# Joining two programs of a Trainium2 kernel into one, with a LayerNorm run by pairs of tiles behind the last residual sums

## The chip, the cores and the metric

The kernel runs on one core of one Trainium2 chip. The metric is the device time of one execution in microseconds; the kernel before takes 2159.62 us (median of 3 runs, 2158.93 to 2162.39). Inside the core TensorE (PE), VectorE (DVE), ScalarE (ACT), GpSimd (POOL) and SyncE (SP, which here issues every DMA) run in parallel and meet at semaphores.

## The reference, cut to what matters

`x` is 1024 tokens (2 batches of 512) by 512. Four residual layers follow each other, each fed by a LayerNorm without weights:

```
x = x + (block-masked linear)(layernorm(x))     # 512 -> 512, with bias
x = x + ffn(layernorm(x))                       # int4-like weights, dequantized by groups of 128
x = x + mixer(layernorm(x))                     # Mamba-2 style, 128 heads of 64
x = x + ffn(layernorm(x))                       # the same weights again

layernorm(x) = (x - mean(x)) / sqrt(var(x) + 1e-5)
ffn(x)   = (silu(x @ Wg) * (x @ Wu)) @ Wd       # W = (q - z) * s, inner width 1792
mixer(x): proj = x @ in_proj.T                  # gate, x, B, C, dt
          dt = softplus(dt + dt_bias); conv of 4 taps and silu on x, B, C
          chunked scan over 4 chunks of 128 tokens; RMS norm, gate, out_proj
```

Inputs of floating type and the output are fp32.

## The kernel before, in words

Tokens are 8 tiles of 128 (`T = 8`), held in SBUF as `xr`. Every product of fp32 accuracy is three fp32r matmuls (`PASSES`: high by high, high by low, low by high), so each operand has a "high" copy, rounded by ACT, and a "low" copy, the remainder, made by DVE or POOL.

There are two programs (`nc.Block`), both written by the function `ffn(name, tiles, dst, lead, ...)`, with a barrier of all engines between them. The first ("f1") leads with the masked linear layer (class `Mixing`) and then runs the FFN; the second ("f2") leads with the mixer (class `Mixer`, 64 steps of the loop over `k`, one pair of heads and one batch each) and then runs the FFN again. In each program every engine has its own list of instructions, in an order written by hand.

The FFN works on 14 tiles of the inner width, two at a time: `PAIRS = 7` bodies. A body has, on PE, gate and up projections of two inner tiles over two halves of the tokens (96 matmuls, L406), then for each token tile t a down projection of 6 matmuls (L417) into one of four banks `dn_bank[t % 4]`. On DVE it has `deq_dn` and `deq_gu` (dequantize the next weights, two passes each, L264, L269, L248, L255), `hidden` (L276, L279) and the eight residual sums `xr += dn_bank` (L303). The down projection of tile t waits until the sum of tile t - 4 has read the bank; in the first body (`first`) only tiles 4 to 7 wait. The first body starts after the norm in front of it, so its DVE list is shifted against the PE's: both `deq_gu(p + 1, ...)` stand before the sums there.

In the last body of f1 each sum is followed by `mixer_stats(t)` (BN_STATS of the tile, L460). SP stores each finished tile to `x_mid` in DRAM (L241) and waits for all eight stores; then the program ends.

The mixer then starts with its own norm: on DVE eight BN_AGGR, the variance, a reciprocal after ACT's square root (L1268, with a table load), and for each tile `m_xn = (x - mean) * rstd` (L1490); PE turns each tile with 4 transposes (`turn_norm`, L1080), ACT makes the high copy (L1262), DVE the low copy (L1475). On PE follow `project_dt(0)` and `project_dt(1)` (L1088, 12 matmuls each) and the projections of the units b, c, x, z (12 matmuls each, `project`, L958). ACT's `tap` (L1214) and three DVE passes (`conv`, L1379) make the convolution of a unit. The chain of `dt` is: DVE adds the bias (L1498), takes -|dt| (L1501), ACT takes exp (L1279) and ln(1 + .) (L1282, another table), DVE forms `dt_h` (L1505), and PE turns it (`turn_dt`, L1097), after which `cumulate` (L1104), the cumulative sums and their stores and loads through DRAM lead to step 0 of the mixer.

The norm inside f1 and f2 already goes by pairs, with helpers of which these are the ones that the change reuses: `norm_var(i)` (two BN_AGGR and the addition of eps, L94 to L98), `norm_root` (ACT square root, L103), `norm_inverse` and `norm_shift` (DVE, L108 and L113), `norm_center_act` (ACT, `x * rstd + shift`, L121), `norm_turn` (PE, L129), `norm_high` (ACT, L135) and `norm_low` (DVE, L141).

Of the kernel before, what the change touches and what calls it, by code (L numbers as in the profile page):

```python
# [5 lines left out]
P = 128  # L6
F32 = mybir.dt.float32
# [40 lines left out]
def build(nc, x_in, mask_t, wa_t, bias_a, w_in, conv_w, conv_b, dt_bias, a_log, d_res, norm_w, w_out,  # L48
          gu_w, gu_z, gu_s, dn_w, dn_z, dn_s, x_mid, e_t, a_parts, out):
    with ExitStack() as ctx:  # L50
# [23 lines left out]
        class Norm:  # L74
            def __init__(self, name, sb, x, banks):
                self.x, self.lnt, self.xn, self.banks = x, None, None, banks
# [40 lines left out]
        def norm_center_act(act, n, t):  # L117
            act.wait_ge(n.stats_done, 7 * (t // 2) + 7)
            if t >= 2:
                act.wait_ge(n.turned, t - 1)  # L120
            nc.scalar.activation(n.xn[:, t % 2], n.x[:, t], ACT.Identity, bias=n.shift[:, t:t + 1],  # L121
                                 scale=n.rstd[:, t:t + 1]).then_inc(n.xn_done, 1)

        def norm_turn(pe, n, t):
            pe.wait_ge(n.xn_done, t + 1)
            if t >= 4:
                pe.wait_ge(n.lo_done, t - 3)
            for k in range(KT):
                last = nc.tensor.transpose(n.banks[t % 4][:, k * P:(k + 1) * P],  # L129
                                           n.xn[:, t % 2, k * P:(k + 1) * P], ident[:])  # L130
            last.then_inc(n.turned, 1)

        def norm_high(act, n, t):
            act.wait_ge(n.turned, t + 1)
            nc.scalar.activation(n.lnt[:, 0, :, t * P:(t + 1) * P],  # L135
                                 n.banks[t % 4][:].rearrange("p (k c) -> p k c", k=KT),
                                 ACT.Copy).then_inc(n.hi_done, 1)

        def norm_low(dve, n, t):
            dve.wait_ge(n.hi_done, t + 1)  # L140
            nc.vector.tensor_tensor(n.lnt[:, 1, :, t * P:(t + 1) * P],  # L141
                                    n.banks[t % 4][:].rearrange("p (k c) -> p k c", k=KT),
# [61 lines left out]
        def ffn(name, tiles, dst, lead, also_load=None, also_after=None):  # L204
# [11 lines left out]
            dn_mm, res_done, stored = sem(name + "_dn_mm"), sem(name + "_res_done"), sem(name + "_stored")  # L216
            g_bank, u_bank, dn_bank = tiles.banks[0:2], tiles.banks[2:4], tiles.banks[4:8]
# [8 lines left out]
            with nc.Block() as block:  # L226
                @block.sync
                def _(sp):
                    lead.sync(sp, tiles)
                    with sp.Fori(1, PAIRS) as p:  # L230
                        for j in range(2):
                            sp.wait_ge(gu_deq, 2 * p + (j - 1))
                            tiles.load_gu(sp, p, j)
                        for j in range(2):
                            sp.wait_ge(dn_deq, 2 * p + (j - 1))
                            tiles.load_dn(sp, p, j)
                    if also_load:
                        also_load(sp)
                    for t in range(T):
                        sp.wait_ge(res_done, (PAIRS - 1) * T + t + 1)  # L240
                        sp.dma_start(dst[t * P:(t + 1) * P, :], xr[:, t]).then_inc(stored, 16)  # L241
                    sp.wait_ge(stored, 16 * T)

                @block.vector
                def _(dve):
                    def sub_gu(p, j):
                        dve.wait_ge(gu_loaded[j], 48 * p + 48)
                        nc.vector.tensor_tensor(gu_q[j][:].bitcast(F32), gu_q[j][:], gu_zr[j][:], ALU.subtract)\  # L248
                            .then_inc(gu_sub, 1)

                    def scale_gu(p, j):
                        dve.wait_ge(gu_sub, 2 * p + (j + 1))
                        if not (isinstance(p, int) and p == 0 and j == 0):
                            dve.wait_ge(gu_lo, 2 * p + j)
                        nc.vector.tensor_tensor(gu_f[:], gu_q[j][:].bitcast(F32), gu_sr[j][:], ALU.mult)\  # L255
                            .then_inc(gu_deq, 1)

                    def deq_gu(p, j):
                        sub_gu(p, j)
                        scale_gu(p, j)  # L260

                    def deq_dn(p, j, first):
                        dve.wait_ge(dn_loaded[j], 48 * p + 48)
                        nc.vector.tensor_tensor(dn_q[:, j].bitcast(F32), dn_q[:, j], dn_zr[:, j], ALU.subtract)\  # L264
                            .then_inc(dn_sub, 1)
                        dve.wait_ge(dn_sub, 2 * p + (j + 1))
                        if not first:
                            dve.wait_ge(dn_lo, 2 * p + j)
                        nc.vector.tensor_tensor(dn_f[:], dn_q[:, j].bitcast(F32), dn_sr[:, j], ALU.mult)\  # L269
                            .then_inc(dn_deq, 1)  # L270

                    def hidden(p, j, half):
                        u = 2 * j + half
                        dve.wait_ge(u_mm, 4 * p + (u + 1))
                        dve.wait_ge(silu_done, 4 * p + (u + 1))
                        nc.vector.tensor_tensor(hf[:, half], silu[:, half], u_bank[half][:], ALU.mult)\  # L276
                            .then_inc(hf_done, 1)
                        dve.wait_ge(h_hi, 4 * p + (u + 1))
# [1477 lines left out]
```

## Time and profile before

| what | value |
|---|---|
| median of 3 runs | 2159.62 us (2158.93 to 2162.39) |
| time of the profiled execution | 2159.47 us |
| its span on the core | 2157.7 us |
| mean granted TensorE clock | 0.993 of full |
| PE busy | 2110.9 us, 98% |
| DVE, ACT, POOL busy | 1693.8, 1393.3, 881.9 us |
| DMA moved | 241.89 MB |

The profile describes one execution. Busy time of PE is not PE at its peak: matmuls at a lower granted clock count as busy too. The masked linear layer and the first FFN take the span up to about 286 us, the mixer up to about 1916 us, the second FFN the rest.

### The profile page before, as it was taken

The numbers are of one execution on the slowest core, as the hardware profiler recorded it, in microseconds if no ns is written. First come the engines' busy times: TensorE is split into PE (matmuls) and PEld (weight loads), VectorE is DVE, ScalarE is ACT, GpSimd is POOL, SyncE is SP. The second block draws the span as 40 slices with busy tenths as digits, with TensorE's granted clock in tenths as the row PEclk, the third lists the DMA queues.
The fourth block names the chain that finished last, engine by engine and source line by source line (L and its number), as shares of the span: only waits on it lengthen the run. The fifth ranks groups of instructions, "written<-read, shape, count | busy, mean of one in ns | idle before, by whom it ended". The sixth has DMA issues, their size and how long they took to land.

```text
span 2157.7 us, 37467 instructions
## 1 busy us (share of the span) xinstructions
PE 2110.9 (98%) x13386; PEld 1736.3 (80%) x13386; DVE 1693.8 (78%) x2682; ACT 1393.3 (65%) x1901; POOL 881.9 (41%) x622
## 2 busy tenths in 40 slices
PE   7999988999999999999999999999999999999999
PEld 6788867788888888888888888888888888877887
DVE  7555467989898888888898889898887988875554
ACT  5322247878787778777787877787777778742221
POOL 1222124445454544454454544544544545422221
PEclk9999989999999999999999999999999999999999
DMA  5544214333333333233323333333333233354441
GB/s 200 164 144 141 68 65 129 113 99 97 109 99 98 109 99 117 95 104 108 99 99 108 103 95 116 104 121 95 99 105 107 92 111 98 112 184 155 138 146 39
DMA packets 128644, 241.89 MB, mean 112 GB/s; under 512 B 14048, under 2 KB 48608, under 8 KB 128224
## 3 DMA queue, kind: packets, MB, share of 16 engines
q1 hardware_dynamic: 128480, 239.73, 35.1%
q8 instruction: 100, 1.64, 0.3%
q14 instruction: 64, 0.52, 0.1%
HBM read 234.17 MB, written 5.51 MB: 111 GB/s over the span
## 4 chain that ended last, share of the span: by engine, by line
PE 80%; DVE 2%; issue 2%; ACT 1%; DMA 1%; POOL 0%; SPq 0%; DVEq 0%; ACTq 0%; POOLq 0%
PE ring L958 35%; PE ring L1058 15%; PE bank_e L406 6%; PE yt L1039 6%; PE st L1023 4%; PE yt L1045 4%; PE bank_e L417 3%; PE xt L1010 3%; PE arg L996 2%; PE xt L971 1%; DMA w_raw<-w_in 0%; PE arg L1088 0%; DVE xc L1379 0%; PE st L983 0%; DVE m_xn L1490 0%
## 5 line engine op out<-in xcount | busy, mean ns | idle before, releaser
L958 PE MATMUL ring<-m_lnt,w_sb 128*128 128x512 f32 x3456 | 860.6, 399 | 1.9 <-DVE xc L1379 1.9
L958 PEld LDWEIGHTS ring<-m_lnt,w_sb 128*128 128x128 f32 x3456 | 632.4, 189 | 129.6 <-DVE xc L1379 2.1
L1643 POOL TENSOR_TENSOR w_sb<-w_raw,w_sb 128x512 fp32r<-128x512 f32 x288 | 401.8, 1400 | 174.1 <-ACT w_sb L1202 173.9
L1658 POOL TENSOR_TENSOR ysq<-ysq,y 128x512 f32<-128x512 f32 x126 | 163.0, 1294 | 654.0 <-ACT y L1246 654.0
L1058 PE MATMUL ring<-wo,ygs 128*128 128x512 f32 x1536 | 369.6, 390 | 2.0 <-issue 2.0
L1058 PEld LDWEIGHTS ring<-wo,ygs 128*128 128x128 f32 x1536 | 287.2, 188 | 63.3 <-issue 2.7
L1379 DVE SCALAR_TENSOR_TENSOR xc<-ring,cw,xc 128x511 f32<-128x511 f32 (+2 forms) x384 | 286.2, 745 | 21.7 <-ACT xc L1214 12.6
L1214 ACT ACTIVATE xc<-ring,cb,cw 128x512 f32<-128x512 f32 x128 | 99.1, 775 | 218.1 <-PE ring L958 218.1
L1648 POOL TENSOR_TENSOR wo<-wo_raw,wo 128x512 fp32r<-128x512 f32 x128 | 214.0, 1672 | 0.0
L1202 ACT ACTIVATE w_sb<-w_raw 128x512 fp32r<-128x512 f32 x288 | 177.1, 620 | 27.5 <-DMA w_raw<-w_in 27.4
L1039 PE MATMUL yt<-em,x_dt 128*64 128x128 f32 x2048 | 183.9, 279 | 3.4 <-DVE state L1421 3.4
L1433 DVE TENSOR_TENSOR ce<-ce,bc 128x768 f32<-128x768 f32 x128 | 176.6, 1380 | 0.0
L1415 DVE COPY state<-st 128x128 f32<-128x128 f32 x128 | 37.3, 291 | 172.8 <-PE st L1023 172.8
L320 POOL TENSOR_TENSOR f_gu<-f_gu_f,f_gu 128x1024 fp32r<-128x1024 f32 x28 | 67.2, 2399 | 252.5 <-ACT f_gu L344 252.5
L1219 ACT ACT_TABLE_LOAD x127 | 162.9, 1283 | 2.3
L1242 ACT ACT_TABLE_LOAD x127 | 162.9, 1283 | 2.3
L1441 DVE TENSOR_TENSOR em<-arg,gt 128x1024 f32<-128x1024 f32 x128 | 155.9, 1218 | 4.0 <-ACT arg L1242 3.9
L406 PE MATMUL bank_e<-f_lnt,f_gu 128*128 128x512 f32 x672 | 154.3, 390 | 1.0 <-DVE f_lnt L141 1.0
L406 PE MATMUL bank<-f_lnt,f_gu 128*128 128x512 f32 x672 | 154.1, 390 | 0.7 <-DVE f_lnt L141 0.7
L1045 PE MATMUL yt<-ce,state 128*64 128x128 f32 x1536 | 149.6, 273 | 0.0
L406 PEld LDWEIGHTS bank_e<-f_lnt,f_gu 128*128 128x128 f32 x672 | 125.9, 188 | 27.4 <-DVE f_lnt L141 1.4
L406 PEld LDWEIGHTS bank<-f_lnt,f_gu 128*128 128x128 f32 x672 | 126.0, 188 | 27.0 <-DVE f_lnt L141 1.1
(199 smaller groups left out, 3167.0 us busy)
## 6 DMA issues: line engine op xcount, KB each, us to landing
w_raw<-w_in SPq DMA_DIRECT2D x288, 256.0 KB, 4.3
ce<-e_t SPq DMA_DIRECT2D x128, 384.0 KB, 4.2
wo_raw<-w_out SPq DMA_DIRECT2D x128, 256.0 KB, 4.4
f_gu_q<-gu_w SPq DMA_DIRECT2D x28, 512.0 KB, 3.8
f_gu_zr<-gu_z SPq DMA_DIRECT2D x28, 512.0 KB, 4.5
f_gu_sr<-gu_s SPq DMA_DIRECT2D x28, 512.0 KB, 5.4
f_dn_q<-dn_w SPq DMA_DIRECT2D x28, 256.0 KB, 3.5
f_dn_zr<-dn_z SPq DMA_DIRECT2D x28, 256.0 KB, 4.2
```

Of the source, the lines that this page charges most:

```text
L406: mm = nc.tensor.matmul(dst[half][:], gu[:, j, b, c:c + P], lnt[:, a, k, half * TOK:(half + 1) * TOK], start=(i == 0), stop=(i == 3 * KT - 1))
L958: mm = nc.tensor.matmul(dst[:], w_sb[:, u % WR, wp, k * P:(k + 1) * P], lnt[:, xp, k, b * S:(b + 1) * S], start=(i == 0), stop=(i == 3 * K ...
L1039: mm = nc.tensor.matmul(YT[h * HD:(h + 1) * HD, c * CS:(c + 1) * CS], x_dt[:, at:at + HD], em[:, h, c * CS:(c + 1) * CS], start=True, stop ...
L1045: mm = nc.tensor.matmul(YT[h * HD:(h + 1) * HD, c * CS:(c + 1) * CS], state[:, c - 1, h * HD:(h + 1) * HD], ce[:, k % 2, h, (c - 1) * CS:c ...
L1058: mm = nc.tensor.matmul(dst[:], ygs[:, j % OR, yp, t * P:(t + 1) * P], wo[:, j % WOR, wp], start=(m == 0), stop=(m == 3 * HALF - 1))
L1202: nc.scalar.activation(w_sb[:, u % WR, 0], w_raw[:, u % NR], ACT.Copy).then_inc(w_hi, 1)
L1219: nc.scalar.activation(xc[:, k % 3], xc[:, k % 3], ACT.Silu).then_inc(silu_x, 1)
L1379: nc.vector.scalar_tensor_tensor(out=dst[:, d:S], in0=src[:, 0:S - d], scalar=cw[:, tile, j:j + 1], in1=dst[:, d:S], op0=ALU.mult, op1=ALU ...
L1433: nc.vector.tensor_tensor(ce[:, k % 2], ce[:, k % 2], c_off.rearrange("p (o t) -> p o t", o=1) .to_broadcast([P, 2, OFFC * CS]), ALU.mult) ...
L1643: nc.gpsimd.tensor_tensor(w_sb[:, u % WR, 1], w_raw[:, u % NR], w_sb[:, u % WR, 0].bitcast(F32), ALU.subtract).then_inc(w_lo, 1)
L1648: nc.gpsimd.tensor_tensor(wo[:, j % WOR, 1], wo_raw[:, j % 2], wo[:, j % WOR, 0].bitcast(F32), ALU.subtract).then_inc(wo_lo, 1)
L1658: nc.gpsimd.tensor_tensor(part, part, y[:, k % 2], ALU.add).then_inc(ysq_done, 1)
```

## The change

There is one program instead of two: `ffn` returns its five lists of instructions, and one `nc.Block` runs f1's and then f2's on each engine. The barrier is gone, and so is SP's wait for the eight stores at the end of f1; SP waits for them (`f1.stored`) before it reads `x_mid` back, DVE before it first writes `acc` (the same memory as `xr`), and POOL waits for the last up projections of f1 before its memsets.

The mixer's norm uses the helpers that go by pairs, with four `xn` buffers and eight banks, and starts inside f1's last body: DVE by `vector_sums`, PE by `tensor_sums` (turns of tiles 0 and 1 ahead of the down projections of tiles 6 and 7). Centering goes from DVE to ACT. The load of `a_log` goes to the early loads of f1. `m_xn` and `wdt` move in SBUF.

In the mixer's beginning, PE has unit b between the turns and `project_dt(1)`, ACT has `tap(("b", 0))` before the exponent of `dt`, and DVE has `conv(("b", 0))` before the bias of the second batch. `dec_done` becomes the fourth count of `rest_done`.

In the first body of both FFNs, DVE makes the sums of tiles 0 to 3 ahead of `deq_gu(p + 1, 1)`.

```diff
 class Norm:
+    def __init__(self, name, sb, x, banks, depth=2):
...
 def norm_center_act(act, n, t):
-            if t >= 2:
-                act.wait_ge(n.turned, t - 1)
+            if t >= n.depth:
+                act.wait_ge(n.turned, t - n.depth + 1)
 def norm_turn(pe, n, t):
-            if t >= 4:
-                pe.wait_ge(n.lo_done, t - 3)
+            if t >= len(n.banks):
+                pe.wait_ge(n.lo_done, t - len(n.banks) + 1)
...
 # ffn, SP
-                    sp.wait_ge(stored, 16 * T)
+                if not following:
+                    sp.wait_ge(stored, 16 * T)
 # ffn, DVE body
-                        if not last:
+                    if not last and not first:
                         deq_gu(p + 1, 1)
+                    def add(t):
+                        dve.wait_ge(dn_mm, T * p + (t + 1))
+                        nc.vector.tensor_tensor(xr[:, t], xr[:, t], dn_bank[t % 4][:], ALU.add)\
+                            .then_inc(res_done, 1)
+                    def added(t):
+                        add(t)
+                        dve.wait_ge(res_done, T * p + (t + 1))
+                    if last and following:
+                        following.vector_sums(dve, added)
+                    else:
+                        for t in range(T):
+                            add(t)
+                            if first and t == 3:
+                                deq_gu(p + 1, 1)
...
+        nm = Norm("m_n", sb, xr, None, 4)
+        nm.banks, nm.lnt, nm.xn = RING + [ARG[:, 0], ARG[:, 1], XT, ST, YT], lnt, m_xn
...
+            def vector_sums(self, dve, added):
+                def total(t):
+                    added(t)
+                    norm_stat(nm, t)
+                def scale(i):
+                    norm_inverse(dve, nm, i)
+                    norm_shift(dve, nm, i)
+                total(0)
+                total(1)
+                norm_var(dve, nm, 0)
+                added(2)
+                scale(0)
+                norm_stat(nm, 2)
+                total(3)
+                norm_var(dve, nm, 1)
+                added(4)
+                scale(1)
+                norm_stat(nm, 4)
+                norm_low(dve, nm, 0)
+                norm_low(dve, nm, 1)
+                total(5)
+                norm_var(dve, nm, 2)
+                norm_low(dve, nm, 2)
+                norm_low(dve, nm, 3)
+                scale(2)
+                total(6)
+                total(7)
+                norm_var(dve, nm, 3)
+                scale(3)
+            def tensor_sums(self, pe, down):
+                for t in range(6):
+                    down(t)
+                norm_turn(pe, nm, 0)
+                norm_turn(pe, nm, 1)
+                down(6)
+                down(7)
+                norm_turn(pe, nm, 2)
+                norm_turn(pe, nm, 3)
...
 # Mixer, PE
-                for t in range(6):
-                    turn_norm(t)
                 project_dt(0)
-                turn_norm(6)
-                turn_norm(7)
+                for t in range(4, T):
+                    norm_turn(pe, nm, t)
+                project(("b", 0))
                 project_dt(1)
-                project(("b", 0))
                 project(("c", 0))
                 project(("x", 0))
                 turn_dt()
 # Mixer, ACT (after wdt)
                 w_high(("b", 0))
-                for t in range(T):
-                    mixer_norm_high(t)
-                    if t == 1:
-                        w_high(("c", 0))
+                w_high(("c", 0))
+                norm_root(act, nm, 0)
+                norm_center_act(act, nm, 0)
+                norm_center_act(act, nm, 1)
+                norm_root(act, nm, 1)
+                norm_high(act, nm, 0)
+                norm_high(act, nm, 1)
+                norm_center_act(act, nm, 2)
+                norm_center_act(act, nm, 3)
+                norm_high(act, nm, 2)
+                norm_high(act, nm, 3)
+                norm_root(act, nm, 2)
+                norm_center_act(act, nm, 4)
+                norm_center_act(act, nm, 5)
+                norm_root(act, nm, 3)
+                norm_center_act(act, nm, 6)
+                norm_center_act(act, nm, 7)
+                for t in range(4, T):
+                    norm_high(act, nm, t)
                 act.wait_ge(a_in, 16)
                 nc.scalar.activation(a_neg[:], a_neg[:], ACT.Exp).then_inc(softplus, 1)
                 w_high(("x", 0))
+                tap(("b", 0))
                 w_high(("z", 0))
                 act.wait_ge(pre_done, B + 1)
                 nc.scalar.activation(low[:], low[:], ACT.Exp).then_inc(softplus, 1)
-                tap(("b", 0))
 # Mixer, DVE
+                for t in range(4, T):
+                    norm_low(dve, nm, t)
+                biased(0)
+                conv(("b", 0))
+                biased(1)
                 dve.wait_ge(pre_done, B)
                 nc.vector.scalar_tensor_tensor(out=low[:], in0=pre[:], scalar=-1.0, in1=pre[:], op0=ALU.mult,
                                                op1=ALU.min).then_inc(pre_done, 1)
-                conv(("b", 0))
 # Mixer, POOL
+                pool.wait_ge(f1.u_mm, 4 * PAIRS)
...
-        ffn("f1", f1, x_mid, Mixing(), load_early, mixer_stats)
-        ffn("f2", f2, out, Mixer())
+        mixer = Mixer()
+        mixing_part = ffn("f1", f1, x_mid, Mixing(), mixer)
+        mixer_part = ffn("f2", f2, out, mixer)
+        with nc.Block() as block:
+            @block.tensor
+            def _(pe):
+                mixing_part[4](pe)
+                mixer_part[4](pe)
...
```

## Rows read from the trace of the kernel before

**Rows 1.** The page: busy time of each engine; one group (busy, mean ns | idle before).

```profile
PE 2110.9 (98%) x13386; PEld 1736.3 (80%) x13386; DVE 1693.8 (78%) x2682; ACT 1393.3 (65%) x1901; POOL 881.9 (41%) x622
...
L320 POOL TENSOR_TENSOR f_gu<-f_gu_f,f_gu 128x1024 fp32r<-128x1024 f32 x28 | 67.2, 2399 | 252.5 <-ACT f_gu L344 252.5
```

**Rows 2.** Stretches of the mixer: start:end, length, busy (count) per engine, clock, DMA.

```profile
400.00:700.00 300.00, 300.00 (x2118) 247.13 (x2117) 257.20 (x409) 230.80 (x311) 147.53 (x105) 1.00 0.34 102
...
1600.00:1900.00 300.00, 298.45 (x2128) 245.46 (x2127) 257.90 (x415) 229.21 (x306) 141.99 (x101) 1.00 0.33 107
```

**Rows 3.** Timeline of PE, first body of f1: start, length, instructions [idle before].

```profile
72.55 5.60 PE L417 MATMUL bank<-f_dn,f_h 128*128 128x512 f32 x24
81.10 7.33 PE L417 MATMUL bank<-f_dn,f_h 128*128 128x512 f32 x24 [2.94 <-DVE xr L303]
```

**Rows 4.** Timeline of DVE over the same gap.

```profile
77.88 1.21 DVE L248 TENSOR_TENSOR f_gu_q<-f_gu_q,f_gu_zr 128x1024 f32<-128x1024 int32 x1
...
80.27 2.47 DVE L303 TENSOR_TENSOR xr<-xr,bank 128x512 f32<-128x512 f32 x4
```

**Rows 5.** Timelines of PE and of DVE, first body of f2.

```profile
1941.28 5.60 PE L417 MATMUL bank_e<-f_dn,f_h 128*128 128x512 f32 x24
1950.22 8.29 PE L417 MATMUL bank_e<-f_dn,f_h 128*128 128x512 f32 x24 [3.33 <-DVE xr L303]
...
1947.00 1.21 DVE L248 TENSOR_TENSOR f_gu_q<-f_gu_q,f_gu_zr 128x1024 f32<-128x1024 int32 x1
```

**Rows 6.** Stretches of 1 us of PE: busy (count), granted clock, DMA share, GB/s.

```profile
82.00:83.00 1.00, 1.00 (x4) 0.50 0.79 262
...
295.00:296.00 1.00, 0.85 (x4) 0.50 0.05 16
```

**Rows 7.** Timeline of PE across the border of the two programs.

```profile
273.37 11.04 PE L417 MATMUL bank<-f_dn,f_h 128*128 128x512 f32 x48
291.16 1.11 PE L1080 MATMUL xt<-ident,m_xn 128*128 128x128 f32 x4 [6.75 <-DVE m_xn L1490]
...
304.75 3.07 PE L1088 MATMUL arg<-m_lnt,wdt 128*128 128x512 f32 x12 [1.57 <-DVE m_lnt L1475]
307.66 8.36 PE L958 MATMUL ring<-m_lnt,w_sb 128*128 128x512 f32 x36
315.86 0.60 PE L1097 MATMUL xt<-ident,dt_h 128*128 128x128 f32 x4
...
338.21 4.42 PE L958 MATMUL ring<-m_lnt,w_sb 128*128 128x512 f32 x12 [1.89 <-DVE xc L1379]
```

**Rows 8.** Timeline of DVE across the border.

```profile
275.57 0.68 DVE L303 TENSOR_TENSOR xr<-xr,bank 128x512 f32<-128x512 f32 x1
...
285.49 0.69 DVE L460 BATCH_NORM_STATS2 m_stats<-xr 128x6 f32<-128x512 f32 x1
...
308.64 1.23 DVE L1501 SCALAR_TENSOR_TENSOR low<-pre 128x1024 f32<-128x1024 f32 x1
311.66 2.32 DVE L1379 SCALAR_TENSOR_TENSOR bc<-ring,cw,bc 128x511 f32<-128x511 f32 x3 [1.79 <-ACT bc L1214]
```

**Rows 9.** Timelines of DVE and ACT in the norm by pairs of f1.

```profile
49.71 0.25 DVE L96 BATCH_NORM_AGGREGATE f_n_mv<-f_n_stats 128x2 f32<-128x6 f32 x2
...
51.65 1.52 ACT L121 ACTIVATE f_xn<-xr,f_n_shift,f_n_rstd 128x512 f32<-128x512 f32 x2 [1.25 <-DVE f_n_shift L113]
54.12 1.09 ACT L135 ACTIVATE f_lnt<-bank 128x512 fp32r<-128x512 f32 x2 [0.95 <-PE bank L129]
```

**Rows 10.** Timeline of ACT in the mixer's beginning.

```profile
310.87 0.76 ACT L1214 ACTIVATE bc<-ring,cb,cw 128x512 f32<-128x512 f32 x1
311.65 1.28 ACT L1282 ACT_TABLE_LOAD   x1
312.94 1.06 ACT L1282 ACTIVATE low<-low 128x1024 f32<-128x1024 f32 x1
```

**Rows 11.** Timeline of SP: the stores of x_mid.

```profile
276.27 9.53 SPq L241 DMA_DIRECT2D x_mid<-xr  x8
```

More of the change, by code:

```diff
@@ L118, in norm_center_act @@
             act.wait_ge(n.stats_done, 7 * (t // 2) + 7)
-            if t >= 2:
-                act.wait_ge(n.turned, t - 1)
-            nc.scalar.activation(n.xn[:, t % 2], n.x[:, t], ACT.Identity, bias=n.shift[:, t:t + 1],
+            if t >= n.depth:
+                act.wait_ge(n.turned, t - n.depth + 1)
+            nc.scalar.activation(n.xn[:, t % n.depth], n.x[:, t], ACT.Identity, bias=n.shift[:, t:t + 1],
                                  scale=n.rstd[:, t:t + 1]).then_inc(n.xn_done, 1)
@@ L202, in load_dn, with ffn @@
                 sp.dma_start(self.dn_sr[:, j], row(dn_s).to_broadcast([P, D])).then_inc(self.dn_loaded[j], 16)
-        def ffn(name, tiles, dst, lead, also_load=None, also_after=None):
+        def ffn(name, tiles, dst, lead, following=None):
             xr, n, lnt = tiles.xr, tiles.n, tiles.lnt
@@ L216, in ffn @@
             dn_mm, res_done, stored = sem(name + "_dn_mm"), sem(name + "_res_done"), sem(name + "_stored")
+            tiles.stored, tiles.u_mm = stored, u_mm
             g_bank, u_bank, dn_bank = tiles.banks[0:2], tiles.banks[2:4], tiles.banks[4:8]
@@ new lines, in sync @@
+            def sync(sp):
+                lead.sync(sp, tiles)
+                with sp.Fori(1, PAIRS) as p:
+                    for j in range(2):
+                        sp.wait_ge(gu_deq, 2 * p + (j - 1))
+                        tiles.load_gu(sp, p, j)
+                    for j in range(2):
+                        sp.wait_ge(dn_deq, 2 * p + (j - 1))
+                        tiles.load_dn(sp, p, j)
+                if following:
+                    following.load_early(sp)
+                for t in range(T):
+                    sp.wait_ge(res_done, (PAIRS - 1) * T + t + 1)
+                    sp.dma_start(dst[t * P:(t + 1) * P, :], xr[:, t]).then_inc(stored, 16)
+                if not following:
+                    sp.wait_ge(stored, 16 * T)
@@ new lines, in gpsimd, with low_gu, low_dn, body @@
+            def gpsimd(pool):
+                def low_gu(p, j):
+                    pool.wait_ge(gu_hi, 2 * p + (j + 1))
+                    nc.gpsimd.tensor_tensor(gu[:, j, 1], gu_f[:], gu[:, j, 0].bitcast(F32), ALU.subtract)\
+                        .then_inc(gu_lo, 1)
+                def low_dn(p, j):
+                    pool.wait_ge(dn_hi, 2 * p + (j + 1))
+                    nc.gpsimd.tensor_tensor(dn[:, j, 1], dn_f[:], dn[:, j, 0].bitcast(F32), ALU.subtract)\
+                        .then_inc(dn_lo, 1)
+                lead.gpsimd(pool, n, low_gu)
+                def body(p, last):
+                    for j in range(2):
+                        low_dn(p, j)
+                    if not last:
+                        for j in range(2):
+                            low_gu(p + 1, j)
+                loops(pool, body)
@@ L427, in build @@
+            return sync, vector, gpsimd, scalar, tensor
         NR, WR, WOR, OR = 2, 4, 2 * HALF - 1, 2 * HALF
@@ L931, in sync @@
                         if k == END_AT - 4 + END_STEP * t:
+                            sp.wait_ge(f1.stored, 16 * T)
                             need(sp, end_done, t)
@@ L1073, in square_sums @@
                     mm.then_inc(ssq_mm, 1)
-                def turn_norm(t):
-                    pe.wait_ge(m_xn_done, t + 1)
-                    if t >= 6:
-                        pe.wait_ge(m_lo, t - 5)
-                    for k in range(KT):
-                        mm = nc.tensor.transpose(LN_BANK[t][:, k * P:(k + 1) * P], m_xn[:, t % 4, k * P:(k + 1) * P],
-                                                 ident[:])
-                    mm.then_inc(m_turned, 1)
                 def project_dt(b):
-                    pe.wait_ge(m_lo, 4 * b + 4)
+                    pe.wait_ge(nm.lo_done, 4 * b + 4)
                     pe.wait_ge(wdt_lo, 1)
```

420 lines of the change are left out of this document (183 added, 237 removed).

## The prediction

> **What bounds the kernel now.** I read the page first: PE is busy for 98% of the span [rows 1], so time can only come from stretches where PE stands still or runs at a lower clock. Then the stretches of the mixer: from 400 to 1900 us, in five of 300 us, PE is busy throughout, at a granted clock of 1.00, with DVE at 86% and POOL at 49% [rows 2]. That part is a queue of PE work which starts when it is let and takes as long as it takes; what shifts its start shifts the end. What is left are three places, read in the timelines of PE and of the engine that it waits for.
>
> The first is the down projection of the first body of f1. Tiles 0 to 3 end at 78.15; tile 4 needs the bank of tile 0, and starts at 81.10 [rows 3]. DVE had that tile's sum in its list behind `deq_gu(1, 1)`, which begins at 77.88; the sums begin at 80.27 [rows 4]. And 24 matmuls that took 5.60 us before the gap take 7.33 after it, since the granted clock is at 0.50 (1.2 GHz) at 82 us [rows 6]. The second is the same place in f2: a gap of 3.33, then 8.29 in place of 5.60, with `deq_gu(1, 1)` at 1947.00 [rows 5]. The third is the border of the programs: PE ends the last down projection at 284.41, stands for 6.75 us, turns tiles as DVE delivers them, and starts the projections at 307.66 [rows 7].
>
> **First pair of sums ahead of the dequantization.** In f1 the sum of tile 0 can begin at 77.88, where L248 began. In the trace PE resumed 0.83 after the sums began (81.10 - 80.27), so it will resume at 78.71: 2.39 us less gap, with 0.56 left. Tiles 5 to 7 need sums 1 to 3, done within 2.47 us [rows 4], ahead of PE's 1.4 us for a tile. With a gap of 0.56 in place of 2.94 I expect no fall of the clock: the gap of 1.57 at 303 us was followed by 12 matmuls in 3.07 us, that is at the full rate [rows 7]. That gives 7.33 - 5.60 = 1.73 more. Sum for f1: 4.12. For f2, with the same distances: 1950.22 - (1947.00 + 0.83) = 2.39, and 8.29 - 5.60 = 2.69: 5.08. What the moved dequantization costs: it begins 2.5 us later, at 80.35, and ends at 82.9; the copies follow, 1.06 on ACT (as the exponent over 1024 columns [rows 10]) and 2.40 on POOL [rows 1], so by 86.5. PE needs them for the second inner tile of body 1, that is after half of its 96 matmuls at 0.23 (11 us), about 95. Cover of 8.7 us, hence nothing. The load behind it on SP's queue (weights of body 2) is 2.5 us later and not needed for 20 us. Together 9.2, bounds: 4.8 if the clock falls anyway, 9.2 as worked out.
>
> **The border.** The wait for the stores and the barrier vanish: the last store was issued at 285.80 [rows 11], and no engine could begin before it had landed. What begins instead is an order of work on three engines, and I walked it with durations of the same kind.
>
> DVE begins at 275.57; eight pairs of sum and BN_STATS take until 286.18, that is 10.6 us [rows 8]. New among them until `scale(3)`: four `norm_var` of about 0.45 (two BN_AGGR 0.25 and a small pass), four `scale` of about 0.35 (two small passes, each less than those two BN_AGGR) [rows 9], and four `norm_low`, each a pass like the 0.69 of BN_STATS but 0.61 from start to start [rows 8]. 10.6 + 1.8 + 1.4 + 2.4 = 16.2, and some 0.4 of hops: `scale(3)` ends at 292.2. DVE, not PE, sets this stretch. PE meanwhile: six down projections until 281.65 (48 in 11.04), turns of tiles 0 and 1 (their centering on ACT ends at 281.4, two in 1.52 [rows 9]: just in time), tiles 6 and 7 until 285.3, turns 2 and 3 until 286.2. `project_dt(0)` needs the fourth `norm_low`, at 288.1: a gap of 1.9, then 2.8 us of matmuls, turns of 4 and 5, small gaps for 6 and 7.
>
> From 292.2: ACT centers tiles 6 and 7 (1.52), makes four high copies (1.09 for two, 2.2) [rows 9], until 296.0; DVE's last low copy is at 296.65. PE has done b by 297.0 and `project_dt(1)` by 299.8, c and x by 305.4 (2.8 us a unit, 8.36 for three [rows 7]). The other branch, on ACT: table load 1.28, the small exponent about 0.3, a weight copy 0.55, tap 0.76 [rows 10]: 298.95. Conv on DVE 2.32, bias 0.7, -|dt| 1.23 [rows 8]: 303.35. ACT: exp 1.06, table load 1.28, ln 1.06 [rows 10]: 306.8. `dt_h`, as long as -|dt|: 308.1. `turn_dt` at 308.2. It was at 315.86 [rows 7], so the border gives 7.7 us up to there. Behind `turn_dt` nothing is reordered; PE, ACT and DVE alternate in a chain there, so the distance stays, except for one thing.
>
> PE then stands from 305.4 to 308.2, 2.8 us, where it did not stand before. The nearest rows are the gap of 2.94, after which 24 matmuls took 1.73 more [rows 3], and the gap of 1.57, after which none did [rows 7]; 2.8 lies near the first. At 338.21, 12 matmuls after a gap of 1.89 in thin work took 4.42 in place of 2.8, 1.6 more [rows 7]. So bounds for this clock are 0 and 2.69 [rows 5], and I take 1.7. It costs in full, as `cumulate` follows right behind unit z on PE. The border: 7.7 - 1.7 = 6.0, bounds 5.0 to 7.7 by these terms.
>
> The Trainium skill bears on this place (TensorE: Matmul & The Clock Gate, Part 4: PE-mode transpose): transposes are said not to count as PE activity in the way matmuls do. The trace agrees: at 295 us PE was busy for 0.85 of the time with turns and the clock was at 0.50 [rows 6]. By the page, the eight turns of dt behind the gap do not help the clock back, which speaks for the 1.7 and against the zero. A second statement speaks against the change: ScalarE: Activation LUTs, What ACT_TABLE_LOAD costs, has some 2.66 us for each switch of a table with its drain. Here the load takes 1.28 and ln starts 0.01 behind it [rows 10]. The new branch has two loads on its path where the old had one; by the page's price the border would give 1.4 less from the second load, by the row it is as summed.
>
> Moves that cost nothing: POOL's memsets (about 4 us) and low copies now end by 282 and are needed from 288; the `a_log` load and the weights of x and z are issued by 291.5 behind the last store, and ACT takes x at 297.6; SP's and DVE's waits for `f1.stored` come long after the stores landed. Centering on ACT in place of DVE adds 6 us to an engine that was waiting there.
>
> **Sum.** 4.1 + 5.1 + 6.0 = 15.2 us. The profiled execution took 2159.47, its span 2157.7, and 1.77 lies around it; the median is 0.15 higher. 2159.5 - 15.2 = 2144.3.
>
> **The rivals.**
> - More comes: the clock stays at 2.4 GHz after the gap of 2.8, and perhaps one of the later falls (at 338 us, 1.6) goes too. 15.2 + 1.7 + 0 to 1.6: 2141 to 2142.6. For it: 2.8 is shorter than either gap that was followed by a fall. Against: it is nearer to them than to 1.57. Chance 0.15.
> - The border gives little: a transfer or the weights' path through SP, ACT and POOL in steps 0 to 3, where PE also has gaps, absorbs the shift, or ACT's longer list comes late with the turns of 0 and 1, which stand in front of tiles 6 and 7 in PE's queue. Then only the two sums count, with 0 to 2 from the border: 2148.3 to 2150.3. For it: the margin at turn 1 is 0.3 us. Against: DVE, not PE, sets the stretch, so PE has 3 us to spare there; the loads shift with their releasers. Chance 0.12.
> - The clock falls in the first bodies although the gap is short: 4.8 in place of 9.2, 2148.7. Against: no gap below 1.5 us in full work was followed by a fall. Chance 0.06.
> - Slower. The loops' engines meet PE in another phase, and in each of the 64 mixer steps a short wait with a fall of the clock appears, as at 338 us, at 1.6 each. From 10 steps on it eats the 15.2; in 20 of the steps the time is 2159.6 - 15.2 + 32 = 2176. Against: from 400 to 1900 the clock is at 1.00 and PE busy [rows 2], and the order there is unchanged. Chance 0.03.
> - No change: the mixer's start waits for something that the trace does not show and that the border hid, and the sums give less than 5. 2155 to 2163. Chance 0.02.
>
> **How the numbers follow.** The forecast, 2144.3, has the remaining 0.62, with its own range 2142.5 to 2147. A measurement of this kernel tells 0.2%, 4.3 us. Faster by more than that: the first four cases, 0.95; within it: the case of no change, 0.02, and a third of the slower rival, in which only some ten steps are hit, together 0.03; slower: the rest of that rival, 0.02. The range goes from 2140.5, the better end of the first rival, to 2150.5, the end of the second.
>
> **What would show it.** In the profile after: the down projections of the first bodies as two groups with a gap near 0.6 and both near 5.6 us; between the last down projection and unit x no gap above 2.2 on PE, `turn_dt` at 304.1 (308.2 less the 4.1 that the first body gives ahead of it; all times of the walk above leave that out); in the mixer from 400 to 1900 the same density. Wrong would be: the fourth low copy later than 288.1 - 4.1 by more than 1 us, a `turn_dt` whose lead over 315.86 shrinks by the first outputs of the mixer, or a clock below 1.00 after 400 us.

## The result, and the profile after

The changed kernel takes 2144.59 us (median of 4, 2142.83 to 2144.86) against 2159.27, the kernel before with a fourth run: ratio 0.9928, interval 0.9911 to 0.9946. Measured again beside experiment e12 it took 2142.66 (5 runs) against 2159.99: 0.992, 0.9906 to 0.9933. The gain is 14.7 us by the first, 17.3 by the second; 15.2 was forecast. The profiled execution took 2142.83, the fastest of the first four, with a span of 2141.1.

The timeline of PE of the kernel after, at the three places:

```profile
72.86 5.60 PE L424 MATMUL bank<-f_dn,f_h 128*128 128x512 f32 x24
79.00 5.70 PE L424 MATMUL bank<-f_dn,f_h 128*128 128x512 f32 x24 [0.54 <-DVE xr L304]
84.54 15.80 PE L412 MATMUL bank<-f_lnt,f_gu 128*128 128x512 f32 x69
...
269.65 8.33 PE L424 MATMUL bank<-f_dn,f_h 128*128 128x512 f32 x36
277.82 1.04 PE L129 MATMUL ring<-ident,m_xn 128*128 128x128 f32 x8
278.61 2.99 PE L424 MATMUL bank<-f_dn,f_h 128*128 128x512 f32 x12
...
284.68 3.02 PE L1134 MATMUL arg<-m_lnt,wdt 128*128 128x512 f32 x12 [2.21 <-DVE m_lnt L141]
...
304.01 1.12 PE L1143 MATMUL xt<-ident,dt_h 128*128 128x128 f32 x4 [2.18 <-DVE dt_h L1540]
...
305.63 3.80 PE L1013 MATMUL ring<-m_lnt,w_sb 128*128 128x512 f32 x12
...
1929.77 5.60 PE L424 MATMUL bank_e<-f_dn,f_h 128*128 128x512 f32 x24
1936.31 5.70 PE L424 MATMUL bank_e<-f_dn,f_h 128*128 128x512 f32 x24 [0.93 <-DVE xr L304]
```

They answer to [rows 3, 5, 7]. The gaps of 2.94 and 3.33 are 0.54 and 0.93, with both groups of down projections near 5.6. At the border PE goes from down projections to turns and on, with a gap of 2.2 in front of `project_dt(0)`, a small one of 0.97 at the turn of tile 6, and one of 2.2 in front of `turn_dt` (L1143), behind which 12 matmuls take 3.80 us. The clock there, by stretches of 1 us of PE (the columns of [rows 6]):

```profile
303.00:304.00 1.00, 0.00 (x0) 0.98 0.00 0
304.00:305.00 1.00, 0.99 (x5) 0.50 0.00 0
...
307.00:308.00 1.00, 1.00 (x5) 0.81 0.18 64
308.00:309.00 1.00, 1.00 (x6) 1.00 0.00 0
```

DVE of the kernel after, in f1's last body: the sums, the statistics and the low copies stand in one row, without idle time until the last pair's square root:

```profile
280.36 1.27 DVE L141 TENSOR_TENSOR m_lnt<-ring,m_lnt 128x512 fp32r<-128x512 f32 x2
...
283.95 0.68 DVE L141 TENSOR_TENSOR m_lnt<-arg,m_lnt 128x512 fp32r<-128x512 f32 x1
...
288.29 0.17 DVE L108 RECIPROCAL m_n_rstd<-m_n_rstd 128x2 f32<-128x2 f32 x1 [0.27 <-ACT m_n_rstd L103]
288.49 0.16 DVE L113 SCALAR_TENSOR_TENSOR m_n_shift<-m_n_mv,m_n_rstd 128x2 f32<-128x2 f32 x1
```

To see which term is worth what, I took distances between the same instructions of both traces (starts; "step k" is DVE's copy of the first state of scan step k):

| from, to | before | after | gain | forecast |
|---|---|---|---|---|
| f1 first body: first down projection to next gate matmul | 15.71 | 11.69 | 4.02 | 4.12 |
| last body: first down projection to turn_dt | 42.49 | 34.36 | 8.13 | 7.7 |
| turn_dt to cumulate (unit z between) | 3.62 | 5.26 | -1.64 | -1.7 |
| cumulate to first scan arguments | 14.27 | 14.08 | 0.19 | 0 |
| first arguments to step 5 | 64.11 | 65.13 | -1.02 | 0 |
| step 5 to step 127 | 1498.73 | 1496.03 | 2.70 | 0 |
| step 127 to f2's first down projection | 44.69 | 45.27 | -0.58 | 0 |
| f2 first body, as the first row | 17.07 | 12.07 | 5.00 | 5.08 |

With -0.30 ahead of the first and 0.10 in the other stretches that is the 16.6 us between the spans. The terms of the edits came as worked out. The 2.70 inside the scan was in no term; the experiments had to find it. Two of the losses belong to the executions and not to the change. The trace of before has the shortest way to step 5 of all 14 traces of this study, and the five others of the old border take 64.9 to 66.0 where after takes 65.13, so the 1.02 is no loss of the change. And behind step 127 the clock of after is at 0.50 for 3.4 us from 1891.2, while in before it stays at 1.00 there; the changed kernel's second trace (e13) has no such fall and takes 44.67, as before does.

### The profile page after: what moved, and what is told of

The parts are those of the page before. It is cut to its first block, busy times and chain, and to the rows that moved or that the text cites. A ratio compares the mean times of both kernels' runs of the same rounds, so it can differ in the third digit from the quotient of the medians.

```text
span 2141.1 us, 37479 instructions
## 1 busy us (share of the span) xinstructions
PE 2103.0 (98%) x13386; PEld 1733.5 (81%) x13386; DVE 1693.5 (79%) x2684; ACT 1398.8 (65%) x1912; POOL 882.4 (41%) x622
## 3 DMA queue, kind: packets, MB, share of 16 engines
q8 instruction: 100, 1.64, 0.3%
## 4 chain that ended last, share of the span: by engine, by line
PE 89%; DVE 4%; issue 3%; ACT 2%; DMA 1%; POOL 1%; SPq 0%; DVEq 0%; POOLq 0%; ACTq 0%
PE ring L1013 35%; PE ring L1113 16%; PE bank L412 6%; PE bank_e L412 6%; PE yt L1094 6%; PE st L1078 4%; PE yt L1100 4%; PE xt L1065 3%; PE bank_e L424 3%; PE bank L424 3%; PE arg L1051 2%; PE xt L1026 1%; PE bank L654 1%; DMA w_raw<-w_in 1%; DVE xr L304 0%
```

## The experiments

**e1, the sums alone, and e2, the border alone.** e1 is the kernel before with the first edit:

```diff
-                        if not last:
+                        if not last and not first:
                             deq_gu(p + 1, 1)
...
+                            if first and t == 3:
+                                deq_gu(p + 1, 1)
```

> The kernel before with the first edit alone: two programs, but in the first body of both FFNs the sums of tiles 0 to 3 stand ahead of the second dequantization. My sum gives 4.1 us in f1 and 5.1 us in f2, 9.2 together, so 2150.1 against 2159.3; the first body's down projections should be two groups of 5.6 to 5.7 us with a gap below 1 us, and the mixer's beginning as before (turn_dt 42.5 us behind the last body's first down projection, as before). The rival that the fall of the clock comes in spite of the short gap gives 4.8 us, 2154.5. The rival that the two parts of the change help each other gives less than 8 us.

Measured: 2153.78 against 2160.46, ratio 0.9967 (0.9955 to 0.9978): 6.7 us and not 9.2, though the interval, 4.8 to 9.7 us, holds both. Both first bodies were as expected, 11.69 and 12.07 us, together 9.0 less than in the trace of before. Yet the spans of the two traces differ by 5.3 only. e1's trace is longer where the edit changed nothing: by 0.9 ahead of the first body, 0.6 up to turn_dt (43.09), 1.3 from the first arguments to step 5 (65.41), and 0.6 behind step 127. Part of the miss is that before's own trace lost more to the clock in the first bodies than others of the old order do, as e6 and its like show below; why those other stretches are longer in e1 is not shown.

e2 is the changed kernel with the first edit taken back:

```diff
-                    if not last and not first:
+                    if not last:
                         deq_gu(p + 1, 1)
...
-                            if first and t == 3:
-                                deq_gu(p + 1, 1)
```

> The changed kernel without the first edit (both dequantizations ahead of all sums again): one program and the norm by pairs alone. The sum of terms gives 6.0 us for it by the prediction, and by the trace of the changed kernel some 5.5 (6.5 up to the first scan step, 1 us lost in steps 0 to 4) and perhaps 2 us more that came slowly over the 128 steps of the mixer: 5.5 to 8, so 2151.3 to 2153.8. The rival that the border gives nothing of its own expects 2157 to 2161. If the slow gain belongs to this part, the mean distance of two matmuls of a mixer projection is 236.5 ns as in the changed kernel and not 237.4 as before.

Measured: 2148.66, ratio 0.9947 (0.993 to 0.9963): 11.8 us, above both. turn_dt came at 34.36, as in the changed kernel, and behind it, PE's timeline of e2:

```profile
307.32 0.66 PE L1141 MATMUL xt<-ident,dt_h 128*128 128x128 f32 x4 [2.02 <-DVE dt_h L1538]
...
308.17 3.01 PE L1011 MATMUL ring<-m_lnt,w_sb 128*128 128x512 f32 x12
```

The gap is there, the fall of the clock is not, so the border gave 8.1 and lost nothing; the slow gain in the scan is in this part too (1498.73 became 1496.03). Three things lift it above the 6.0: the slow gain of 2.7, the clock that stayed up behind the gap, and first bodies that, in the old order, lost 2.6 us less here than in the trace of before (14.09 and 16.10). 6.7 and 11.8 add to 18.5, against 14.7 and 17.3 for the whole; by the spans of the traces it is 5.3 and 11.2 against 16.6. The two parts do not depend on each other beyond what the intervals leave open.

**e3, one program without the overlap.** In `vector_sums` and `tensor_sums`:

```diff
-                total(0)
...
-                scale(3)
+                for t in range(T):
+                    added(t)
+                for i in range(4):
+                    norm_stat(nm, 2 * i)
+                    norm_stat(nm, 2 * i + 1)
+                    norm_var(dve, nm, i)
+                    if i == 2:
+                        norm_low(dve, nm, 0)
+                        norm_low(dve, nm, 1)
+                    if i == 3:
+                        norm_low(dve, nm, 2)
+                        norm_low(dve, nm, 3)
+                    scale(i)
...
-                for t in range(6):
+                for t in range(T):
                     down(t)
                 norm_turn(pe, nm, 0)
                 norm_turn(pe, nm, 1)
-                down(6)
-                down(7)
```

> The changed kernel, but the norm is not among the residual sums of f1's last body: DVE makes all eight sums first and then the four pairs, and PE makes all eight down projections ahead of the first turns. It keeps one program, the helpers and the first edit. Theory: the gain of the border is the overlap of the norm with the sums; DVE has then about 12.6 us of norm work behind the last sum where the changed kernel has 7, so turn_dt comes about 5 us later and the time is near 2149.5. Rival: the gain comes from the barrier and the wait for the stores that are gone; then this kernel is within 1.5 us of the changed one, 2143 to 2146.

Measured: 2151.23, ratio 0.9958 (0.9941 to 0.9974); turn_dt at 43.74, later than before (42.49). PE's timeline of e3:

```profile
270.42 11.04 PE L424 MATMUL bank<-f_dn,f_h 128*128 128x512 f32 x48
285.60 1.97 PE L129 MATMUL ring<-ident,m_xn 128*128 128x128 f32 x8 [4.14 <-ACT m_xn L121]
...
294.96 4.79 PE L1123 MATMUL arg<-m_lnt,wdt 128*128 128x512 f32 x12 [4.04 <-DVE m_lnt L141]
```

PE waits for the norm twice, at a low clock (the 12 matmuls in 4.79), with neither the barrier nor the wait for the stores in its way. What e3 has against before comes from its first bodies and the scan. So one program with the norm behind all the sums does not give the gain of the border; the norm has to stand among the sums. My 5 us of delay were too few (9.4): the late norm also cost the clock and a second wait.

e3 does not tell what the barrier was worth. It puts all eight BN_STATS behind the last sum, two in 1.28 us, where the kernel before had seven of them among the sums: e3 overlaps less than before did. DVE's timeline of the kernel before shows its wait at the border:

```profile
287.92 0.64 DVE L1481 BATCH_NORM_AGGREGATE m_mv<-m_stats 128x2 f32<-128x6 f32 x8 [1.74 <-PEq L226]
```

These 1.74 us are gone in the changed kernel. How the 8.1 us divide between them and the new order is not shown; a kernel with one program and the old order was not run.

**e5, the turns behind tile 7**, which asks who sets the stretch:

```diff
-                for t in range(6):
+                for t in range(T):
                     down(t)
                 norm_turn(pe, nm, 0)
                 norm_turn(pe, nm, 1)
-                down(6)
-                down(7)
```

> The changed kernel with the turns of tiles 0 and 1 behind the down projections of tiles 6 and 7 on PE; DVE's and ACT's lists as in the changed kernel. Theory: DVE sets this stretch, and its low copies of tiles 0 and 1 stand in front of the sums of tiles 5 to 7. The turns come 2.8 us later, the first low copy waits for them (280.36 becomes about 282.5), and as DVE has no slack, scale(3) and turn_dt come 2 to 2.5 us later; the time rises by 2 to 2.5 us. Rival: PE sets the stretch, so that the order of turns and down projections makes no difference: turn_dt within 0.5 us of 34.4 us behind the last body's first down projection.

DVE's timeline of e5:

```profile
282.02 1.29 DVE L141 TENSOR_TENSOR m_lnt<-ring,m_lnt 128x512 fp32r<-128x512 f32 x2 [1.36 <-ACT m_lnt L135]
```

The first low copy came 12.15 us behind the first down projection (269.87) in place of 10.71, so 1.44 later, and turn_dt 35.82 behind it in place of 34.36, so 1.46 later: DVE has no slack there, and the delay arrives whole. It is smaller than the 2 to 2.5 expected, since DVE had reached its wait only after 1.4 of the 2.8 us. The single time, 2143.02 against 2163.02, shows none of it: here too unit z ran at the full clock (3.70 to cumulate, 5.26 in the changed kernel), which is 1.6 us the other way.

**e6 and e8, the addresses.** In the trace of the changed kernel the scan gained 0.022 us a step, evenly from step 5 on, with PE busy throughout. Matmuls of the projections followed each other in 236.5 ns on average (successive starts inside a unit, 500 to 1800 us) where they took 237.3 before. The new `Norm` has 128 bytes a partition more than `m_stats`, and lies ahead of `w_raw`, `w_sb` and most of the mixer's tiles in SBUF. e6 and e8 are the kernel before with 128 unused bytes at that place:

```diff
         m_stats = sb("m_stats", [P, T, 6])
+        sb("pad", [P, 32])
```

> The kernel before with an unused tile of 128 bytes a partition behind the statistics, which moves w_raw, w_sb, m_lnt and all later tiles to the addresses they have in the changed kernel. Theory: the slow gain of 2.7 us over the mixer's steps comes from these addresses; then the mean distance of two matmuls of a mixer projection is 236.5 ns in place of 237.4, and the time is about 2.5 us below that of before. Rival: it belongs to the order or the phase of the engines, or differs from chip to chip; then it is 237.4 here and the time is that of before.

> The same kernel as e6 (before, with all tiles from w_raw on 128 bytes higher), now timed. Theory: the 2.8 us that its trace showed over the mixer's steps are there in every execution: ratio 0.9982 to 0.9992, 2156.5 to 2158.5 against 2160. Rival: it was that execution's: ratio 0.9995 to 1.0005.

e6: step 5 to 127 in 1496.04, mean distance 236.5; 2156.38 (one run, against one of before at 2163.02, the highest that before ever had, so the times say little). e8: 2156.77 (11 runs) against 2159.6, ratio 0.9986 (0.9977 to 0.9995): 2.8 us. e8's trace has 1495.94 and 236.5. The whole of the slow gain is this shift, and the theory in e8 holds.

The same two kernels have the sums in the old order. PE's timeline of e6:

```profile
73.94 5.60 PE L417 MATMUL bank<-f_dn,f_h 128*128 128x512 f32 x24
82.48 5.71 PE L417 MATMUL bank<-f_dn,f_h 128*128 128x512 f32 x24 [2.94 <-DVE xr L303]
```

This is the gap of 2.94 of [rows 3], and no fall of the clock behind it. Of the six traces with the old order (before, e2, e6, e8, e10, e11) the first body of f1 took 15.7 in three and 14.1 in three; the one of f2 took 17.07 before and 16.07 to 16.11 in the five others.

**e10 and e11, which address.** e10 puts the 128 bytes behind `w_sb`, e11 takes 64 bytes (`[P, 16]`) at e6's place:

```diff
         w_sb = sb("w_sb", [P, WR, 2, KT * P], F32R)
+        sb("pad", [P, 32])
```

> Before, with the 128 unused bytes behind w_sb, so that the projection's weights stay where they were and its activations m_lnt and the mixer's other tiles move. If the activations' address is the cause, the mean distance of two projection matmuls is 236.5 ns as in e6; if the weights' address is, it stays at 237.3.

> Before, with 64 unused bytes in place of e6's 128 at the same place. If any shift away from the addresses of before helps, the mean distance is 236.5 ns or below; if only some do, it may be 237.3 or above. No theory of mine says which.

PE alone between 500 and 1800 us, one row each of before, of the kernel after, of e6 and of e10 (length, busy, matmuls, clock, DMA):

```profile
500.00:1800.00 1300.00, 1299.43 (x9101) 1.00 0.34 104
```

```profile
500.00:1800.00 1300.00, 1299.43 (x9119) 1.00 0.33 104
```

```profile
500.00:1800.00 1300.00, 1299.43 (x9113) 1.00 0.33 104
```

```profile
500.00:1800.00 1300.00, 1299.47 (x9043) 1.00 0.33 103
```

PE is equally busy at a clock of 1.00 in all four, and gets through more or less. e10: 239.2 ns, step 5 to 127 in 1507.80, 9 us longer than before; 2168.97 in its one run, against 2159.6. e11: 236.5 ns, 1495.96, 2157.6. So neither of my two outcomes for e10 came. Moving all tiles by 64 or 128 bytes gives the same 236.5; leaving the weights where they were and moving the rest costs. That the two operands of a matmul must lie well to each other does not explain it all. The output projections (`wo`, `ygs`) follow each other in 226.9 ns in before, 226.8 in e6 and 228.9 in e10, and make 2.6 of the 9 us; yet both of their operands are allocated behind the unused bytes in e6 and in e10, at the same places. What differs between e6 and e10 is the place of `w_raw` and `w_sb` alone. So the place of tiles that a matmul does not read can matter too; which accesses meet where was not tried.

**e4, e7 and e12, the gap in front of turn_dt.** e4 exchanges two lines of PE's list:

```diff
-                turn_dt()
                 project(("z", 0))
+                turn_dt()
```

> The changed kernel with the projection of unit z 0 ahead of turn_dt on PE, so that it fills the gap of 2.2 us there. Theory: the gap costs its fall of the clock (12 matmuls in 3.8 us in place of 2.8) and the wait itself; filled, turn_dt starts 0.6 us later, the clock stays at 1.00, and cumulate starts 1.5 to 2.5 us earlier than 39.6 us behind the last body's first down projection; the time is 2142 to 2143.2. Rival: the chain of dt on ACT and DVE sets the rest and PE's order does not matter: 2144 to 2146.

2143.58, ratio 0.9921 (0.9905 to 0.9938). turn_dt at 34.77, cumulate 1.38 behind it, that is 36.15 in place of 39.62, more than the 1.5 to 2.5 expected, but the first arguments at 53.17 in place of 53.70. The time lies between the theory's range and the rival's. ACT's timeline of e4 shows who took over:

```profile
309.38 1.06 ACT L1273 ACTIVATE bc<-bc 128x1024 f32<-128x1024 f32 x1 [1.63 <-DVE bc L1431]
310.34 1.06 ACT L1343 ACTIVATE cum<-arg 128x512 f32<-128x512 f32 x2
```

ACT's copy of the sums, ready since 308.6, stands behind the silu of b and c, which waits for a convolution. e7 is e4 with the copies first:

```diff
-                activate_bc(0)
                 for b in range(B):
                     act.wait_ge(cum_mm, b + 1)
...
+                activate_bc(0)
```

> The kernel of e4 (unit z 0 ahead of turn_dt), and on ACT the two copies of the cumulative sums ahead of the silu of b and c. In e4 cumulate began 1.38 us behind turn_dt, yet the first scan step came 17.02 us behind it in place of 14.1, since ACT's copy stood behind the silu, which waits for the convolution of c. Theory: with the copy first the chain starts about 1.9 us earlier, the first scan step comes 15.0 to 15.5 us behind cumulate, 51.0 to 51.7 us behind the last body's first down projection (53.7 in the changed kernel), and the time is 1 to 2.5 us below that of the changed kernel: 2142 to 2143.5. Rival: the DMAs of the scan arguments or the silu that now comes later take the place of the copy, and it stays at 52.5 to 53.5 and 2143.5 to 2145.

2141.6 (5 runs), ratio 0.9917 (0.9903 to 0.993). The time lies 0.4 below the theory's range and 1.9 below the rival's, and the changed kernel, too, came lower when it was measured again (2142.66). The distance is not the theory's: 34.76 + 1.38 + 16.41 = 52.55, the rival's. On DVE both convolutions stand ahead of `diff`, DVE's timeline of e7:

```profile
309.45 2.31 DVE L1431 SCALAR_TENSOR_TENSOR xc<-ring,cw,xc 128x511 f32<-128x511 f32 x3
311.67 1.93 DVE L1552 TENSOR_TENSOR diff<-cum 128x1024 f32<-128x1024 f32 x1
```

e12 is e7 with the parts reordered on both engines:

```diff
 # ACT
+                nc.scalar.activation(parts[:, 0], ...)
                 activate_bc(0)
                 w_high(("x", 2))
-                nc.scalar.activation(parts[:, 0], ...)
                 activate_x(0)
-                nc.scalar.activation(e_end[:], ...)
-                act.wait_ge(rest_done, 2)
+                act.wait_ge(rest_done, 1)
                 nc.scalar.activation(parts[:, 1], ...)
-                act.wait_ge(rest_done, 1)
-                nc.scalar.activation(diff[:], ...)
+                nc.scalar.activation(e_end[:], ...)
                 act.wait_ge(rest_done, 3)
                 nc.scalar.activation(parts[:, 2], ...)
+                nc.scalar.activation(diff[:], ...)
 # DVE: rest, diff, rest, dt_q in place of diff, rest, dt_q, rest
```

> The kernel of e7, with the three parts of the cumulative sums brought forward in ACT's and DVE's lists: the first part ahead of the silu of b and c, the second ahead of the table load and e_end, the third ahead of the exponent of diff, and on DVE the first remainder ahead of diff and the second ahead of dt_q. In e7 DVE's convolution and diff had taken the place of ACT's wait. Theory: this chain (cumulate, parts, stores, arguments) sets the first scan step; the distance from the last body's first down projection to the first arguments falls from 52.55 to 50.6 to 51.4, and the time to 1 to 2 us below that of e7, that is 3 us below the changed kernel where the clock falls as often. Rival: the first scan step waits for the decays (dec_q), which come later here, or PE's queue; then it stays at 52 to 53.

2141.57, ratio 0.9915 (0.9902 to 0.9929): as e7, and not 1 to 2 us below it. 52.15 to the first arguments is the rival's range again. The chain of e12 has in the place of the parts:

```profile
316.55 0.95 ACT diff L1354
317.50 0.96 ACT e_cum L1355
318.47 0.32 SPq L967
```

The exponent `e_cum` is now last, and its store stands on SP's queue ahead of the loads of the arguments. Neither the theory nor the rival named it, and no run moved it, so that it sets the rest is argued from this chain alone. e7 and e12 are the fastest kernels of this study, and both are clearly faster than the kernel before; against the changed kernel (2142.66 beside e12) the difference of about 1 us is within the intervals.

**e13, the changed kernel again.**

> The changed kernel once more, on the chip and in the minutes of e12, as its yardstick: 2143 to 2145, ratio 0.992 to 0.9935. In its trace the distances of the first edits are as before (11.7 and 12.1 us for the first bodies, 34.4 to turn_dt); whether unit z behind turn_dt takes 2.8 or 3.8 us (3.70 or 5.26 from turn_dt to cumulate) tells whether the clock falls in that gap in every execution: it did in the changed kernel's and not in those of e2, e3 and e5 with gaps of 1.7 to 2.1.

2142.66, a little below the range, ratio inside it. Its distances are 11.69, 34.36 and 12.07. turn_dt to cumulate 5.28, and PE's row behind the gap (2.18, as in the first trace):

```profile
305.58 4.60 PE L1013 MATMUL ring<-m_lnt,w_sb 128*128 128x512 f32 x12
```

The clock fell both times in the changed kernel with a gap of 2.18, and in none of e2, e3 and e5 with gaps of 2.02, 1.73 and 2.06. Two of two against none of three is a hint that the gap's length matters, not more. e4, e7 and e12 have no such gap there.

## Why the prediction was right, and where it was not

**First pair of sums.** Right in mechanism and, against the profile of before, in size: 4.02 and 5.00 for 4.12 and 5.08. But the terms for the clock, 1.73 and 2.69, were those of one execution. In the six traces with the old order f1 lost nothing to the clock in three, and f2 lost 1 us less than in before's trace in the five others. The waits, 2.4 us each, are in all. Taking the middle of f1's two values and f2's usual one, the edit is worth (14.9 - 11.7) + (16.1 - 12.1) = 7.2, and e1 measured 6.7 (4.8 to 9.7). The dequantization moved behind the sums cost nothing, as forecast: between the first body and the last 185.11 us in both kernels.

**The border.** The walk gave turn_dt at 34.83 behind the first down projection (308.2 - 273.37) and it came at 34.36. The fourth low copy ended at 15.0 behind it (284.63 - 269.65), where the walk had 14.7. That DVE sets the stretch is shown by e5, that one program with the norm behind the sums gives nothing up to turn_dt by e3; how much of the gain is the barrier's is open. The clock term had the right size in the changed kernel (1.64 for 1.7) and is 0 in e2. Its reasoning had luck: it put the gap at 2.8 us, near the 2.94 of [rows 3], and the gap was 2.18, no longer near it; and 2.94 itself was followed by a fall in three traces of six only.

**The table load.** The new branch has two. Exp's and ln's took 1.28 each in the kernel after, and ln started 0.01 behind its load; no drain of the length that the Trainium skill gives (ScalarE: Activation LUTs, What ACT_TABLE_LOAD costs) appears in the rows, ACT's timeline of the kernel after:

```profile
299.27 1.06 ACT L1332 ACTIVATE low<-low 128x1024 f32<-128x1024 f32 x1 [3.79 <-DVE low L1537]
300.35 1.28 ACT L1334 ACT_TABLE_LOAD   x1
301.64 1.06 ACT L1334 ACTIVATE low<-low 128x1024 f32<-128x1024 f32 x1
```

**The scan.** Expecting "in the mixer from 400 to 1900 the same density" is where the prediction was wrong: the moves in SBUF and the larger statistics were put at nothing, and 128 bytes were worth 2.8 us (e8). This was missing from the sum, and the clock terms of the first bodies were about 2 too large. That 2144.3 lies 0.3 from the first median is in part luck, since the two errors cancel. By the second median it is 1.6 off.

**The rivals.** "More comes" is near the second median, but not by its mechanism: the clock fell behind the gap in both traces of the changed kernel, and fell again near 327 us. "The border gives little" is refuted by e2. The slower rival spoke of 64 scan steps; there are 128 (64 pairs of heads, two batches). The range's ends, 2140.5 and 2150.5, are not quite those of the rivals named for them, 2141.0 and 2150.3 by their own terms. The bound of 10 steps stands, and no step between 400 and 1885 us shows a fall:

```profile
400.00:700.00 300.00, 300.00 (x2111) 247.51 (x2111) 257.79 (x413) 229.70 (x310) 148.17 (x105) 1.00 0.32 102
...
1600.00:1885.00 285.00, 284.35 (x2016) 234.26 (x2014) 246.32 (x393) 218.19 (x291) 134.08 (x96) 1.00 0.33 108
```

What stays open: why the stretch to step 5 varies from 64.1 to 66.7 between traces. It holds one or two falls of the clock that come at other moments each time, 3.4 us at 0.50 in all in e6 and 6.8 in before, but e6 takes longer (64.92 against 64.11), so the falls alone do not order it. By the prediction's own sign of being wrong, a lead of turn_dt that shrinks, 1.02 us went here, but against a trace of before that is the shortest of all.

## What to carry to other kernels

Where two stages meet, write down for each engine what stands in its list between the last work of the one and the first of the other, and interleave on the engine that is full in that stretch: here one program with the norm left behind the sums gained nothing up to turn_dt (e3). A wait that an order causes is worth its length for certain and the clock behind it only sometimes: price the two apart, and look at more than one trace. After each link that is shortened in a chain over five queues, look which list holds the next one: e4 was to bring 1.5 to 2.5 us, e7 1.5 to 2.2 and e12 1.2 to 1.9, and they gave 0.5, 0.6 and 0.4 at the first arguments.

## What the runs showed of the hardware that was not expected

Where tiles lie in SBUF changes the rate of matmuls at the full clock: 236.5, 237.3 or 239.2 ns from start to start for the same 128x512 matmuls of the projections, with 64 or 128 unused bytes ahead of the weights and all later tiles, none, or 128 behind the weights. The scan is 2.7 us shorter or 9 longer by it, and busy time does not show it; the count of matmuls in a fixed stretch does. e10 slowed even matmuls whose own operands had not moved against e6 (226.8 to 228.9 ns). And the same gap of 2.94 us in front of the same matmuls was followed by a stretch of 3.4 us at 1.2 GHz in three of six traces and by none in the others.
